# The low halves of two experts' second weights are made on GpSimd instead of VectorE

## The reference

```
x = x + gnn(layernorm(x))        # 2500 nodes x 512, 80000 edges
x = x + moe(layernorm(x))

gnn: h = x + segment_sum(x[src], dst);  relu(h @ W1 + b1) @ W2 + b2

moe: gate = softmax(x @ Wg)               # 8 experts, the best 2 of each node
     scores = top-2 of gate, made to sum to 1
     for e in range(8):
         h  = gelu(x @ W1[e] + b1[e])     # 512 -> 256
         out += (h @ W2[e] + b2[e]) * scores[:, e]   # 256 -> 512
```

## Time and profile before

| what | before |
|---|---|
| median of 3 runs | 602.82 us |
| lowest and highest | 597.49, 604.74 us |
| the profiled execution | 601.47 us |
| its span, first to last instruction | 599.7 us |
| mean granted clock of TensorE | 0.978 of full speed |
| busy: PE, DVE, ACT, POOL | 88%, 75%, 51%, 45% of the span |

### The profile page before, as it was taken

One profiled execution on the slowest core, in us unless ns is written; L12 is line 12 of the kernel. 1 busy time (PEld: TensorE's weight loads), 2 busy tenths in 40 slices (PEclk: granted clock), 3 DMA queues, 4 the chain that ended last, 5 costly groups with the idle time before them and its releaser, 6 DMA issues.

```text
span 599.7 us, 13973 instructions
## 1 busy us (share of the span) xinstructions
PE 526.0 (88%) x4766; PEld 392.7 (65%) x4767; DVE 452.0 (75%) x977; ACT 304.4 (51%) x577; POOL 272.3 (45%) x251
## 2 busy tenths in 40 slices
PE   5899888999999999999999989739898888879970
PEld 3798788566566576666666646627677767667750
DVE  4979999774899999999993367898875656555672
ACT  3786776342533754565446223644764555444561
POOL 7463223030531351324215173436876666675743
PEclk9999999999999999999999999969999999998995
DMA  8437100300413432251234134968987678766765
GB/s 253 143 102 203 61 1 3 82 1 2 116 50 98 136 110 88 87 175 71 88 106 157 51 102 86 318 227 282 265 153 131 125 134 140 133 120 130 126 91 70
DMA packets 40361, 72.27 MB, mean 120 GB/s; under 512 B 12571, under 2 KB 16801, under 8 KB 39761
## 3 DMA queue, kind: packets, MB, share of 16 engines
q0 software_dynamic: 11840, 26.06, 23.2%
q1 hardware_dynamic: 21779, 32.36, 17.7%
q10 hardware_dynamic: 6680, 13.06, 6.6%
HBM read 43.97 MB, written 29.06 MB: 122 GB/s over the span
## 4 chain that ended last, share of the span: by engine, by line
PE 65%; DVE 15%; issue 5%; another core or an unknown queue 4%; ACT 4%; DMA 4%; SPq 1%; POOL 1%; ACTq 0%; POOLq 0%; DVEq 0%
PE psum L1664 20%; PE psum L1712 9%; PE psum L1846 7%; PE psum L1836 7%; PE psum L1648 6%; PE psum L1671 6%; PE psum L1578 5%; DVE hot_lo L1229 2%; DMA bound_rows<-in_dst,chunk_i 2%; ACT he L987 2%; PE psum L1813 2%; DVE hot_key L1229 1%; DVE he_hi L1498 1%; DMA dst_i<-in_dst 1%
## 5 line engine op out<-in xcount | busy, mean ns | idle before, releaser
L786 ACT ACTIVATE counts<-psum 128x400 bf16<-128x400 f32 x125 | 61.5, 507 | 101.6 <-PE psum L1648 99.5
L1229 DVE TENSOR_TENSOR hot_lo<-iota_lo,lo_w 128x1024 f16<-128x1024 f16 x125 | 103.3, 826 | 0.0
L725 POOL DMA_INDIRECT out_x<-y,target_i x47 | 78.4, 1669 | 48.2 <-DVE y L1509 31.7
L1229 DVE TENSOR_TENSOR hot_key<-iota_key,key_w 128x800 f16<-128x800 f16 x125 | 84.2, 674 | 18.0 <-PE psum L1648 17.2
L987 ACT ACTIVATE he<-psum,eb_col,up_undo 128x128 f32<-128x128 f32 x94 | 42.5, 457 | 78.5 <-PE psum L1836 51.6
L1664 PE MATMUL psum<-counts,z_hi 125*128 125x500 bf16 x320 | 80.6, 373 | 0.9 <-SPq L513 0.9
L1664 PE MATMUL psum<-counts,z_lo 125*128 125x500 bf16 x320 | 80.5, 374 | 0.0
L1648 PEld LDWEIGHTS psum<-hot_key,hot_lo 128*128 128x128 f16 x1000 | 55.2, 97 | 27.3 <-ACT counts L786 4.6
L1648 PE MATMUL psum<-hot_key,hot_lo 128*128 128x100 f16 x1000 | 63.6, 207 | 6.8 <-ACT counts L786 3.7
L695 POOL TENSOR_TENSOR x_res<-x_res,b_row 125x512 f32<-125x512 f32 x19 | 30.8, 1630 | 80.3 <-DMA x_res<-in_x 80.3
L719 POOL DMA_INDIRECT xg<-xt_d,token_i x47 | 51.1, 1087 | 21.2 <-issue 12.2
(11 more groups left out here) (295 smaller groups left out, 1212.5 us busy)
## 6 DMA issues: line engine op xcount, KB each, us to landing
out_x<-x SPq DMA_DIRECT2D x20, 224.0 KB
xt_d<-xt SPq DMA_DIRECT2D x20, 224.0 KB
x_res<-in_x SPq DMA_DIRECT2D x19, 224.0 KB
up_raw<-in_L_ffn_W ACTq DMA_DIRECT2D x8, 512.0 KB, 4.2
up_d<-up_split ACTq DMA_DIRECT2D x8, 512.0 KB
w_both<-up_d SPq DMA_DIRECT2D x8, 512.0 KB, 5.2
w_raw<-in_L_ffn_W SPq DMA_DIRECT2D x8, 512.0 KB, 6.9
W_raw<-in_L_gnn_W ACTq DMA_DIRECT2D x2, 1024.0 KB, 5.2
```

Source lines behind the costliest of these rows:

```text
L725: pool.indirect_dma_start(out=out[:, :], in_=y[:, k % YB], in_offset=None, out_offset=bass.IndirectOffsetOnAxis(ap=target_i[:, k:k + 1], a ...
L786: act.activation(counts[:, it % 2, :, place:place + W], psum[:, WIN + w % 2, 0:MW].rearrange("p (w h) -> p h w", w=W), ACT.Copy).then_inc( ...
L1229: ins = dve.tensor_tensor(hot[:, w % RING].rearrange("p s (n two) -> p s n two", two=2), iota[:].rearrange("p (o n two) -> p o n two", o=1 ...
```

## The change

GpSimd makes `w2_lo[1]` and `w2_lo[2]`, with the same subtraction, after its last `low_rows` and ahead of the first gather. It waits for `w_hi_ready` to count their high halves. VectorE no longer makes these two. The low half of expert 3 keeps its place in block 2, now behind a wait for the first three counts of `w_lo_ready`. Those of experts 0 and 4 to 7 stay as they are.

```
--- before.py
+++ after.py
@@ -712,6 +712,9 @@
                 rest_of_sum(g, 3)
             for q in range(4):
                 low_rows(G - 1, q)
+            for e in (1, 2):
+                pool.wait_ge(S["w_hi_ready"], e + 1)
+                pool.tensor_tensor(w2_lo[e][:], w2_raw[e][:], w2_hi[e][:].bitcast(F32), ALU.subtract).then_inc(S["w_lo_ready"], 1)
 
             def gather(k):
                 if k >= XB:
@@ -1463,7 +1466,6 @@
             turned_low(0)
             step(dve.scalar_tensor_tensor(empty[:], node_at[:], 0.0, lane[:, 0:NT], ALU.is_equal, ALU.mult))
             step(dve.tensor_tensor(target_i[:], token_f, empty[:], ALU.add))
-            split_low(1)
             dve.wait_ge(S["slots_spread"], SCORES_SPREAD)
             step(dve.tensor_scalar(score_low[:], psum[:, 6, NT:2 * NT], 1.0 / SCALE, None, ALU.mult))
             dve.scalar_tensor_tensor(slot_score[:], psum[:, 6, 0:NT], 1.0 / SCALE, score_low[:], ALU.mult, ALU.add)\
@@ -1502,8 +1504,9 @@
                     turned_low(k + 1)
                 if k == 0:
                     landings()
-                if 1 <= k < AHEAD - 1:
-                    split_low(k + 1)
+                if k == 2:
+                    dve.wait_ge(S["w_lo_ready"], 3)
+                    split_low(3)
                 dve.wait_ge(S["bias_scaled"], k + 1)
                 dve.wait_ge(S["down_done"], k + 1)
                 dve.scalar_tensor_tensor(y[:, k % YB], psum[:, 4], slot_score[:, k:k + 1], y[:, k % YB], ALU.mult, ALU.add).then_inc(S["y_taken"], 1)
```

## The result

| | before | changed |
|---|---|---|
| median (lowest to highest) | 601.90 us (597.49 to 604.74), 4 runs | 610.71 us (609.16 to 613.74), 4 runs |
| the profiled execution, its span | 601.47, 599.7 us | 609.35, 607.6 us |
| mean granted clock of TensorE | 0.978 | 0.968 |

The ratio is 1.0141, with a 95% interval from 1.0095 to 1.0186: 8.5 us, between 5.7 and 11.2, slower (the two medians as they stand differ by 8.8). That is inside 2%, as forecast, but above the range of 601 to 610. The forecast was right about the stretch it looked at hardest and missed a second loss of about the same size, 6 us further on, behind the first gather.

The account below looks back on a forecast made before the run. The prediction took VectorE's chain to the first gather as the bound: the profiled 601.47 + 4.2 for VectorE's waits - 0.1 for the removals = 605.6, 606.9 on the median; it predicted 606, range 601 to 610.

Parts of the forecast that it names:

- GpSimd's own length: Ahead of the first gather: two subtractions of 2.40 us each, 4.8 in all, 5.1 at most, fitting before 399.95.
- What they do to VectorE: Ahead of the first gather: second `at_row_last` and `ends_before` each wait 2.2 us for GpSimd's subtractions, 4.2 taken in all.
- It fits beside VectorE: Rival ahead of the first gather: VectorE is hardly held up, removals give 0.1 to 2.4 us; chance 0.12.
- Half the price: Rival ahead of the first gather: one subtraction collides or TensorE's wait swallows part, +1 to +2.5 us; chance 0.18.
- The subtraction removed before `score_low`: 1.22 us on VectorE, worth nothing: Block 0: removing it from VectorE gains nothing, since ACT's first gelu and TensorE's second layer cover its 1.22 us.
- What follows from it: From `token_i` and the first gather on, everything moves together by +4.2 us, which goes through to the end.
- The subtraction removed in block 1: At 414.60: 1.22 us off VectorE is worth 0.1; GpSimd's first add gets 1.0 shorter, gaining nothing.
- The blocks fall into a worse rhythm: Rival in the blocks from 440 on: five more unnamed ACT waits of 1.9 us, slower by over 2%; chance 0.04.

Follow-up runs that it names:

- e6: e4 with GpSimd making the low halves of experts 2 and 3 after the eight first gathers, not VectorE in blocks 1 and 2; 1.0027 to the kernel before.
- e1: Changed kernel with VectorE's subtraction for expert 3 moved from block 2 to the removed subtraction's place behind `target_i`; 605.51 us, 1.0076 to the kernel before.
- e12: e1 with each of GpSimd's two subtractions in four pieces of 128x256; 604.45 us, 1.0041 to the kernel before.
- e2: Kernel before with VectorE's subtraction for expert 1 moved from behind `target_i` into block 0, none on GpSimd; 605.06 us, 1.0062 to the kernel before.
- e4: Kernel before with each GpSimd add also waiting for TensorE's first layer of the following block; 597.20 us, 0.9944 to the kernel before.
- e3: Changed kernel with the fifth of the eight first gathers waiting for TensorE's first layer of block 0; 609.66 us, 1.0135 to the kernel before.
- e8: Changed kernel with a small GpSimd memset ahead of each of the last five of the eight first gathers; 608.27 us, 1.0068 to the kernel before.
- e10: Kernel before with each GpSimd add waiting for TensorE's transposes of the block after the next; 587.08 us, 0.9752 to the kernel before.

## Why the prediction was wrong, step by step

**GpSimd's own length** was 2.56 each, 2.40 forecast from the fit on columns; 5.1 in all, inside the bound. In e6, where VectorE stood, they took 2.32 each. Right enough.

**What they do to VectorE**, the step that was to decide, was right: +2.2 each forecast, +2.01 and +2.02 measured, on the two instructions named. The sum 3.86 stands against 4.2; e1 prices it alone at 4.6 us (2.7 to 6.4). The trace has GpSimd hold VectorE for the rest of its instruction; the exclusive lock of the Trainium skill, page "SBUF — State Buffer", section "SBUF: two separate sides", says the same, and the size agrees (2.0 of 2.56, the rest had passed when VectorE came). "It fits beside VectorE" and "Half the price" are thereby out for two subtractions. e12 shows the turn-taking of the earlier trace rows, at 0.4 to 0.5 us a turn. e6 shows a case where VectorE got no turn between two of them, 4.89 under 4.64; why it got none there I leave open.

**The step that failed is "The subtraction removed before `score_low`: 1.22 us on VectorE, worth nothing".** I looked for who waits for that subtraction (ScalarE and TensorE, neither) and not for whom it made wait. It held GpSimd's fifth gather by 0.8 us. Its removal costs 3.7 us by e2, with no other part of the change present, and the brake put back, with the collision still there, brings the price from 1.0141 to 1.0076 (e1). With it fails the sentence in "What follows from it", that nothing behind was lost: the chain did not move as one piece, since between first gather and first `y` 3.9 us were added.

The clue stood in rows I had used: I took 1.0 us off the first add because it had run beside a subtraction of VectorE, and didn't ask what the same effect did to a gather.

**The subtraction removed in block 1**: the add fell from 2.67 to 1.70 as forecast, and nothing came of it, as forecast.

**"The blocks fall into a worse rhythm"** had the right kind of wait, the unnamed one of the earlier trace rows, and the wrong place and number: not five more of 1.9 in the blocks, where there are two fewer, but one of 5 to 6 ahead of them. The eleven are about every third of the 35 blocks, not every second. I called these waits tied to the blocks; they are tied to GpSimd's issues, and a gate of one line took eleven of them away (e4).

**The range** of 601 to 610 carried the scatter of the median and every rival to the low side. The high side had only a rhythm with 0.04.

**What is shown and what isn't.** That the late signals belong to GpSimd's issues is shown by five edits that each moved or spaced the issues (e1, e3, e4, e8, e10) and by one that took only the brake away (e2). That other engines' signals pass meanwhile is shown by e8's trace. By which way the issue of a transfer keeps TensorE's signals, and TensorE's own next instructions, no run here shows; nor whether it is the issue itself or the traffic of the transfer behind it, though the eleven waits end with the issue. The match in time isn't exact either: in the wait that ends at 489.64, TensorE is done at 487.87, 0.30 before the add's recorded start. Nor is every signal under an issue late: in the kernel before the first gelu starts at 407.16, 0.48 after the half layer that it needs (406.68), while the fifth gather, the one held back by VectorE, is being issued (405.98 to 407.74). That the brake lets signals pass is shown, why it does is not.

## What to carry to other kernels

An instruction off the critical path can be worth its time by whom it blocks: before taking it away, look at what ran beside it and was longer than its kind. When an engine waits for a cause the profile can't name, lay its wait beside GpSimd's indirect transfers and see whether both end together; if so, space them or gate them by TensorE's signals, and try more than one gate, since here one was worth 0.6 and 0.8% and another 2.5%. Work moved to GpSimd beside VectorE's two-table instructions is paid on VectorE, too: 2.0 us here for each subtraction that took VectorE itself 1.2.

## What was not expected of the hardware

- Signals of TensorE reached ScalarE 5.7 and VectorE 5.4 us after the matmuls' end under five indirect gathers in close order, each 0.95 with 0.30 between. With 0.6 between (e8) they came 0.6 (VectorE), 1.5 and 2.5 us (ScalarE) after it, while signals of ScalarE and VectorE passed in 0.05 us or less.
- Around one indirect add, 1.6 to 1.7 us to issue, ScalarE waited 1.8 to 2.2 us for them.
- A subtraction of VectorE over two tables stretches GpSimd's issue of a gather from 0.96 to 1.76 and of an add from 1.70 to 2.67. On the same page of the Trainium skill, section "Who interferes with whom", a `tensor_tensor` is said not to have stalled a transfer in a probe, with the reason marked as inferred; these rows speak against it.
- TensorE issued five pieces of one turn over 4.3 us in that stretch, and its clock then fell to 0.54; it had stood at 1.00 in the kernel before.
